# One score matmul over both halves of k for a head's first tile, and the two halves of o joined later in the step

## The reference

```python
x = x + layernorm(attention(layernorm(x), Wq, Wk, Wv, Wo))      # 16 heads of 64, rotary q and k, causal softmax
x = x + layernorm(ffn(layernorm(x), A, B, Wr, br))              # 8 low-rank experts, softmax router
```

```python
logits = jnp.einsum('bhqd,bhkd->bhqk', q, k)
logits = jnp.where(causal, logits, MASK_VAL) / jnp.sqrt(64)
out = jnp.einsum('bhqk,bhkd->bhqd', softmax(logits), v)
```

## Time and profile before

| | us |
|---|---|
| median of 3 runs | 1069.33 (1069.21 to 1069.33) |
| the profiled execution's own time | 1069.58 |
| its span (first to last instruction) | 1067.8 |

### The profile page before, as it was taken

One profiled execution on the slowest core, in us unless ns is written; L12 is line 12 of the kernel. 1 busy time (PEld: TensorE's weight loads), 2 busy tenths in 40 slices (PEclk: granted clock), 3 DMA queues, 4 the chain that ended last, 5 costly groups with the idle time before them and its releaser, 6 DMA issues.

```text
span 1067.8 us, 20069 instructions
## 1 busy us (share of the span) xinstructions
PE 1049.9 (98%) x5559; PEld 871.3 (82%) x5559; DVE 756.9 (71%) x2138; ACT 591.3 (55%) x1390; POOL 439.4 (41%) x422
## 2 busy tenths in 40 slices
PE   7999999999999999999999999999999999999996
PEld 6888888888888888888888888888877888888884
DVE  8777777776666666666666666666766877777777
ACT  7556666666555665565555655555576333333334
POOL 4153443435353635444452625344457232333221
PEclk9999999999999999999999999999999999999999
DMA  7022324241311256021111112020333323322311
GB/s 280 36 84 70 128 69 128 74 129 55 104 51 34 95 182 227 10 71 33 52 49 31 52 29 69 10 69 17 87 132 93 108 88 107 118 99 87 109 61 60
DMA packets 58663, 90.36 MB, mean 85 GB/s; under 512 B 3568, under 2 KB 36336, under 8 KB 58608
## 3 DMA queue, kind: packets, MB, share of 16 engines
q1 hardware_dynamic: 58464, 89.44, 25.9%
q10 hardware_dynamic: 144, 0.26, 0.1%
HBM read 64.52 MB, written 25.17 MB: 84 GB/s over the span
## 4 chain that ended last, share of the span: by engine, by line
PE 90%; DVE 3%; issue 2%; ACT 2%; POOL 0%; DVEq 0%; ACTq 0%; POOLq 0%
PE bank L1472 46%; PE bank L1403 25%; PE bank L1499 6%; PE bank L1518 3%; PE bank L1517 3%; PE bank L1633 2%; PE bank L1610 1%; PE bank L1445 1%; PE bank L1634 1%; PE bank L1520 1%; PE bank L1433 1%; ACT prob L740 1%; DVE prob L1053 0%; DVE k_hh L1092 0%; PE bank L1415 0%
## 5 line engine op out<-in xcount | busy, mean ns | idle before, releaser
L595 POOL TENSOR_SCALAR prob<-prob,rinv 128x128 f32<-128x128 f32 (+3 forms) x256 | 150.5, 588 | 436.8 <-DVE rinv L1063 436.8
L1472 PE MATMUL bank<-big_hi,w_hi 128*128 128x512 f32 (+1 forms) x776 | 329.4, 424 | 0.3 <-DVE big_lo L1034 0.3
L740 ACT ACTIVATE prob<-prob,nmax 128x128 f32<-128x128 f32 (+3 forms) x256 | 144.0, 562 | 304.3 <-DVE nmax L1053 302.7
L1472 PE MATMUL bank<-big_hi,w_lo 128*128 128x512 f32 (+1 forms) x776 | 304.5, 392 | 0.0
L1472 PE MATMUL bank<-big_lo,w_hi 128*128 128x512 f32 (+1 forms) x776 | 302.1, 389 | 0.0
L1472 PEld LDWEIGHTS bank<-big_hi,w_lo 128*128 128x128 f32 x776 | 145.6, 188 | 33.2
L1071 DVE TENSOR_TENSOR pT_lo<-bank,pT_hi 128x128 fp32r<-128x128 f32 (+3 forms) x256 | 123.7, 483 | 56.0 <-ACT pT_hi L751 53.3
L1472 PEld LDWEIGHTS bank<-big_hi,w_hi 128*128 128x128 f32 x776 | 146.6, 189 | 16.5 <-issue 0.4
L1472 PEld LDWEIGHTS bank<-big_lo,w_hi 128*128 128x128 f32 x776 | 147.1, 190 | 11.6
L1063 DVE RECIPROCAL rinv<-rsum 128x1 f32<-128x1 f32 x256 | 40.8, 159 | 129.3 <-ACT prob L740 128.9
L1053 DVE CUSTOM_DVE_ANT_0 prob<-bank,mask 128x128 f32<-128x128 f32 (+3 forms) x256 | 124.1, 485 | 9.2 <-PE bank L1403 5.1
(11 more groups left out here) (146 smaller groups left out, 1927.7 us busy)
## 6 DMA issues: line engine op xcount, KB each, us to landing
w_raw<-in_wqkv SPq DMA_DIRECT2D x48, 512.0 KB, 4.4
attention_out<-o_sum SPq DMA_DIRECT2D x64, 128.0 KB, 2.3
w_raw<-attention_out SPq DMA_DIRECT2D x16, 512.0 KB, 4.8
land<-in_x SPq DMA_DIRECT2D x16, 512.0 KB, 3.7
out<-res SPq DMA_DIRECT2D x14, 512.0 KB, 2.6
xin<-in_x SPq DMA_DIRECT2D x12, 512.0 KB, 5.7
xT_hold_hi<-xin SPq DMA_DIRECT2D x8, 512.0 KB, 3.6
xT_hold_lo<-xn SPq DMA_DIRECT2D x8, 512.0 KB, 5.4
```

The source lines that it names most:

```text
L595: pool.tensor_scalar(p, p, rinv[:, q % 4:q % 4 + 1], 1.0, ALU.mult, ALU.mult).then_inc(prob_done, 1)
L740: act.activation(prob[:, q % 4, 0:n], prob[:, q % 4, 0:n], ACT.Exp, scale=-1.0, bias=nmax[:, q % 4:q % 4 + 1], accum_out=rsum[:, q % 4:q % ...
L1472: done = pe.matmul(grp_ps[(b + k) % 2][:, cols], w, xt[:, cols], start=at == 0, stop=at == GROUP_MM - 1)
```

## The change

- `k_hh` and `k_lo` become two parts of one tile `k_all`. For q mod 4 = 0 (a head's first tile, 128 columns) `scores` makes one matmul of 256 columns: the moving operand takes 128 columns from `k_hh` and 128 from `k_lo`, and the two products lie side by side in `sc_ps[0]`, columns 0 to 127 and 128 to 255.
- VectorE must now add them. Before such a tile's minimum, `negate` adds the second product and the mask into a new tile `low_masked`, and the minimum takes `low_masked` in place of the mask; it waits for that sum (`low_added`).
- On ScalarE, `o_lower` stands behind `pt_high` in steps 1 and 5, where it stood ahead of it.
- On VectorE, `o_add` stands behind `invert` and `pt_low` in steps 1 and 6, where it stood ahead of both. In the two slots behind the last unit, step 1 already had that order.

```diff
--- before.py
+++ after.py
@@ -136,8 +136,8 @@
 
 
         q_hl = sb(sB, "q_hl", [P, 2, 2, SEQ], F32R)
-        k_hh = sb(sB, "k_hh", [P, 2, 2, SEQ], F32R)
-        k_lo = sb(sB, "k_lo", [P, 2, 2, SEQ], F32R)
+        k_all = sb(sB, "k_all", [P, 2, 2, 2, SEQ], F32R)
+        k_hh, k_lo = k_all[:, 0, :, :, :], k_all[:, 1, :, :, :]
         w_sum = sb(sB, "w_sum", [P, EMBED])
         rope = sb(sB, "rope", [P, SEQ])
         rot = sb(sB, "rot", [P, SEQ])
@@ -153,6 +153,7 @@
         rinv = sb(sB, "rinv", [P, 4])
         o_low = sb(sB, "o_low", [DH, SEQ])
         o_sum = sb(sB, "o_sum", [DH, 2, SEQ])
+        low_masked = sb(sB, "low_masked", [P, P])
 
         hold_hi = xin[:, 1, :].rearrange("p (c t) -> p c t", c=KC)
         hold_lo = xn[:, 1, :].rearrange("p (c t) -> p c t", c=KC)
@@ -222,6 +223,7 @@
         qk_lo_done = sem("qk_lo_done")
         s_done = sem("s_done")
         neg_done = sem("neg_done")
+        low_added = sem("low_added")
         exp_done = sem("exp_done")
         inv_done = sem("inv_done")
         prob_done = sem("prob_done")
@@ -808,15 +810,15 @@
                     exponent(u, s)
                     if s == 0 and real(u - 1):
                         v_raw(u - 1, 1 - b)
-                    if s == 1 and real(u - 2):
-                        o_lower(u - 2, 0)
-                    if s == 5 and real(u - 2) and not (isinstance(u, int) and u > UNITS):
-                        o_lower(u - 2, 1)
                     if s == 2 and real(u - 1):
                         v_high(u - 1, 1 - b, fill)
                     if prepares(u, ahead) and s == 6:
                         ln_start(ahead_tile(u) + 1)
                     pt_high(u, s)
+                    if s == 1 and real(u - 2):
+                        o_lower(u - 2, 0)
+                    if s == 5 and real(u - 2) and not (isinstance(u, int) and u > UNITS):
+                        o_lower(u - 2, 1)
                     if real(u):
                         if s == 0 and b == 0 and late(n, 1):
                             w_high(2, n)
@@ -1050,7 +1052,13 @@
                     if late(g, 4):
                         dve.wait_ge(t_done, g - 3)
                     dve.sem_inc(gate_dve, 1)
-                    dve.tensor_tensor_reduce(prob[:, q % 4, 0:n], sc_ps[q % 2][:, 0:n], mask[:, SEQ - n:SEQ],
+                    added = mask[:, SEQ - n:SEQ]
+                    if q % QT == 0:
+                        added = low_masked[:, :]
+                        dve.tensor_tensor(added, sc_ps[0][:, P:2 * P], mask[:, SEQ - P:SEQ], ALU.add).then_inc(low_added, 1)
+                        dve.wait_ge(low_added, 2 * a + q // QT + 1)
+                        dve.sem_inc(gate_dve, 1)
+                    dve.tensor_tensor_reduce(prob[:, q % 4, 0:n], sc_ps[q % 2][:, 0:n], added,
                                              -SOFT, 3e38, ALU.add, ALU.min, nmax[:, q % 4:q % 4 + 1]
                                              ).then_inc(neg_done, 1)
 
@@ -1134,10 +1142,6 @@
                         if s in (3, 6):
                             rotate(u, b, s // 6)
                     closing = isinstance(u, int) and u >= UNITS
-                    if s == 1 and real(u - 2) and not closing:
-                        o_add(u - 2, 0)
-                    if s == 6 and real(u - 2) and not (closing and u > UNITS):
-                        o_add(u - 2, 1)
                     leads = ahead or (isinstance(u, int) and u == UNITS - 1)
                     if leads and s == 7:
                         k_low(u, b, 0)
@@ -1149,8 +1153,10 @@
                     pt_low(u, s)
                     if s == 0 and not closing and real(u - 1):
                         k_low(u - 1, 1 - b, 1)
-                    if closing and s == 1 and real(u - 2):
+                    if s == 1 and real(u - 2):
                         o_add(u - 2, 0)
+                    if s == 6 and real(u - 2) and not (closing and u > UNITS):
+                        o_add(u - 2, 1)
                     if real(u):
                         if s in (4, 5):
                             q_low(u, b, s - 4)
@@ -1484,9 +1490,13 @@
                     if late(g, 2):
                         pe.wait_ge(neg_done, g - 1)
                     qc, kc = slice(P * i, P * i + P), slice(0, P * i + P)
-                    products(sc_ps[q % 2][:, kc], [(q_hl[:, ab, h, qc], k_hh[:, ab, h, kc]),
-                                                   (q_hl[:, ab, h, qc], k_lo[:, ab, h, kc])], True, True
-                             ).then_inc(s_done, 1)
+                    if i == 0:
+                        pe.matmul(sc_ps[0][:, 0:2 * P].rearrange("p (a n) -> p a n", a=2), q_hl[:, ab, h, qc],
+                                  k_all[:, :, ab, h, kc], start=True, stop=True).then_inc(s_done, 1)
+                    else:
+                        products(sc_ps[q % 2][:, kc], [(q_hl[:, ab, h, qc], k_hh[:, ab, h, kc]),
+                                                       (q_hl[:, ab, h, qc], k_lo[:, ab, h, kc])], True, True
+                                 ).then_inc(s_done, 1)
 
             def turn_probs(u, s):
                 a, q, g = trailing(u, s, 3)
```

## The result

| | before | after |
|---|---|---|
| median, us | 1069.27 (1069.13 to 1069.33) | 1083.41 (1083.11 to 1083.53) |
| ratio to before | | 1.0132 [1.0114, 1.015] |
| the profiled execution's own time, us | 1069.58 | 1083.53 |
| its span, us | 1067.8 | 1081.7 |

A forecast was written before the change was run, and what follows sets the result against it. The softmax chain on VectorE and ScalarE was taken as the bound. Preparing pairs +3.8 and +1.2, late pairs -0.8, used-up lead -0.5: together +3.7 us, 1073.0 us beside the median; range 1066.5 to 1078.

The forecast's parts named there:

- the chain: Softmax steps on VectorE and ScalarE, minimum to next minimum; claimed 48.25 us per pair of slots beside TensorE's 48.32.
- The first rival: TensorE is the bound after all, VectorE absorbs the additions, 6.1 us come out: 1063.2 us; chance 0.12.
- Step 1: o_add of head 0: VectorE does reciprocal and pT_lo first, then waits for o_low; +0.30 us with the addition.
- step 5: o_low of head 1: pT_hi starts 0.74 us earlier; -0.30 with the addition, -1.0 in slots 12 to 29 with b = 1.
- the race: Slots 12 to 29, b = 1: VectorE's q_hl comes before GpSimd's w_sum, taking 0.9 us instead of 1.58; -0.70.
- step 6: o_add of head 1: o_sum leaves VectorE's wait for ScalarE and follows pT_lo; next minimum 0.58 us later.
- part 3: Order around the addition, per slot: pairs preparing second-half tiles +1.27 us, pairs in slots 12 to 29 about -0.1.
- the odd slot's cover: Slots 12 to 29, b = 1: ScalarE's weight conversion before the exponential gives 0.96 us, hiding the 0.58 wholly.
- the addition: 64 VectorE additions the minimum waits for: 0.29 us plus 0.15 waiting, 0.44 per head; bounds 0.21 and 0.6.
- The second rival: The addition costs only 0.21 us, pairs in slots 12 to 29 fall to TensorE's 47.94: 1068.2 us; chance 0.15.
- the third rival: The 2.57 us copy of k_hh, held by GpSimd's w_lo, wins its race: some 2 us less, 1071.0; chance 0.15.
- The fourth rival: q_hl (b = 1) or the k_hh copy loses its race: 0.7 us more per pair, slots 12 to 29, 1079; chance 0.13.

The follow-up runs named there:

- the fast versions: Changed kernel with o_add of head 0 in step 2, of head 1 ahead of the reciprocal: 1062.30 us; also head 0's addition a step earlier: 1060.55 us.

## Why the prediction was right in direction and wrong in size

**Right: what bounds the kernel.** That a saving on TensorE is paid out only as far as the chain gets shorter was the reading all else rested on. The merge without the addition came out at no change, the moves alone at 4.2 us faster with no matmul saved, and in the changed kernel the matmuls saved show as waits at the transposes. The first rival, TensorE as the bound, is out.

**Right: where the costs lie.** Step 1, step 5 in all kinds of slot, the race that `q_hl` wins in odd late slots (0.84 us, not 1.58), and `o_sum` taken out of a hole in step 6 (0.60 by the run that puts it back, 0.58 with `o_low` from partition 0) came as forecast within 0.07 us. The row of that race in the changed kernel:

```profile
608.16 0.84 DVE L1093 TENSOR_TENSOR q_hl<-rot,q_hl 64x512 fp32r<-64x512 f32 x1
```

**Wrong, the main step: part 3 took ScalarE's overlap as given.** "Three steps matter" was false: there was a fourth, step 2, at +0.14, and step 6 cost 0.72 and not 0.58 for the same reason. I had moved `o_lower` and counted whom it makes wait, but not what it does to the instruction that now follows it; the 0.12 us of lost overlap stood in the earlier trace rows. Per pair this is four times 0.14, 0.56 us, and over four preparing and nine late pairs 7.3 us. The run with `o_lower` at partition 0 shows the mechanism. It takes away more than this sum, since it also spares `o_low`'s own late start in step 1, which the kernel before pays too, and 2.2 us in the last slots and behind them.

**Wrong, small: the odd slot's cover.** The earlier trace rows gave 0.96 us of cover ahead of the exponential, and I let it hide all of step 6. It did hide 0.59. The other 0.13 came through, since `pT_hi` itself is late by that much and ScalarE's conversion, which ends the cover, stands behind it. A cover hides what is late on one engine only if what makes the cover isn't late with it. This 0.13 is part of the four times 0.14 above.

**Mis-sized: the addition.** 0.44 was forecast, 0.46 to 0.49 measured: 0.29 for the instruction and 0.19 or 0.20 of waiting for the engine's own result, 12.8 us in 64 times, where I had taken 0.15 from the earlier trace rows. At four per pair this is 0.15 us, 2 us in all. The second rival is out. The sentence of the Trainium skill (VectorE: DVE Perf Modes, section The DRAIN you can't avoid) that in a chain of operations the semaphore costs nothing extra doesn't carry over to a wait for the engine's own last result: that cost 0.19 or 0.20 us at 62 of 64 places here, 0.32 and 0.56 at the other two.

**Mis-sized, without effect: the matmul.** 0.095 was taken, 0.108 measured, nearly the upper bound of 0.11. In the changed kernel TensorE isn't the bound and it changes nothing; the difference is worth 0.05 us per pair in the fast versions.

**Came true beside the forecast: the third rival.** The long copy of the earlier trace rows is gone. In the changed kernel it is

```profile
322.40 0.72 DVE L1100 CAST k_all<-k_all 64x512 fp32r<-64x512 f32 x1
```

and step 7 of slot 11 takes 3.45 us in place of 6.30, of which 0.58 is the cover: some 2.3 us less, about the price that the rival had. The forecast hadn't counted it, so its own terms were short by as much more than the times show. That is luck inside the miss.

**The fourth rival: not in the late slots, but elsewhere.** `q_hl` won its race in the odd late slots. Two collisions did get longer. `q_hl` in the odd preparing slots takes 1.33 to 1.55 us, where it took 0.98 to 1.28. The prediction had that: it comes earlier and still ends behind `w_sum`. The other is new and stands in the next paragraph.

**Put at nothing: the ends.** For the last slots and what follows the sum has no term, and it is +2.5: 1.25 in the last pair of slots and 1.27 from the last score matmul on. In the last slots it goes with the addition (317.6 with it against 315.1 without, in the same order). From the last score matmul to the end it takes 253.5 us before, in the merge with the old order and in the merge without addition, 253 with the moves alone, but 254.2 to 254.8 in every version that has both the addition and moved work. Some 0.8 us of that stands at one place. TensorE's matmul over `ar_sum` (a column sum for the second part) needs GpSimd's `ar_sum`, and VectorE has an operation with two SBUF inputs (`ar_hl`) near it. GpSimd, VectorE and TensorE, before and then changed:

```profile
827.31 0.48 POOL L652 TENSOR_TENSOR ar_sum<-ar_four 128x136 f32<-128x136 f32 x1
...
827.94 1.28 DVE L1178 TENSOR_TENSOR ar_hl<-ar_raw,ar_hl 128x1088 fp32r<-128x1088 f32 x1
...
828.48 0.40 PE L1403 MATMUL bank<-big_lo,w_hi 128*128 128x512 f32 x1
828.71 0.40 PE L1620 MATMUL bank<-ar_sum,ones 128*128 128x136 f32 x2
```

```profile
840.88 1.60 POOL L654 TENSOR_TENSOR ar_sum<-ar_four 128x136 f32<-128x136 f32 x1
...
840.86 1.28 DVE L1184 TENSOR_TENSOR ar_hl<-ar_raw,ar_hl 128x1088 fp32r<-128x1088 f32 x1
...
841.55 0.40 PE L1409 MATMUL bank<-big_lo,w_hi 128*128 128x512 f32 x1
842.58 0.47 PE L1630 MATMUL bank<-ar_sum,ones 128*128 128x136 f32 x2 [0.63 <-issue]
```

`ar_sum` takes 1.58 to 1.62 us in all eight versions with both, where `ar_hl` starts within 0.03 us of it, and 0.48 in the other five, where `ar_hl` starts 0.17 us or more behind it. TensorE's matmul starts 1.03 behind its predecessor and not 0.23. Why the addition and the moved work bring the two starts together, and where the remaining 0.4 to 0.5 us between the last score and that matmul go, stays open.

Together: the preparing stretch was 3.2 us short, the late pairs 4.4, the ends 2.5 and the start 0.2, which is the 10.2 us by which the span missed. The range missed as well. It had been built from the rivals' prices, each a large event with a place, while most of the error was one of a tenth of a microsecond at four places of each pair, all with the same sign. Nothing in the range stood for that.

## What to carry to other kernels

When an instruction is moved, read the two instructions that get new neighbours as well as the one that moves: on the same engine, look at whether each still overlaps the one ahead of it, and from which partitions it and the last reader of PSUM read. Multiply any term by how often it occurs before calling it small: 0.14 us, four times a pair, was 7 us. And work that is taken off a critical chain (here an addition, made a step early) must ask for its input no earlier than the other engine has it, or what stands behind it in the order pays.

## What the runs showed of the hardware

- ScalarE: a PSUM operand that starts at partition 64 behind one at partition 0, or the reverse, loses the overlap of 0.09 us with its predecessor and starts 0.02 to 0.03 us after its end. In the changed kernel `v_hl` does so with the exponential and its accumulator read between it and `o_low`. Taking it away in three places of each slot was worth over 13 us of 1083.
- VectorE: the minimum that waits for the sum made just ahead of it sits idle for 0.19 or 0.20 us in 62 of 64 cases; with another two instructions between, the wait costs nothing.
- VectorE and GpSimd: a VectorE operation with two SBUF inputs that comes in the midst of a GpSimd `w_lo` of 2.42 us ended 0.5 us after it, at 2.09 us of its own where it takes 0.69 alone. The other way round, GpSimd's `ar_sum` of 0.48 us took 1.58 to 1.62 in the eight runs in which VectorE's `ar_hl` (1.28 us, two SBUF inputs) started within 0.03 us of it.
- TensorE: a single 256-column matmul in place of two of 128 columns with the same weights saves 0.108 us, with a moving operand in two runs of 128 columns from two places.
